# GCN passes: node columns looked up on TensorE from a table in two float32r parts instead of three bf16 parts

## The reference

```python
def gcn_conv(x, w, b, row, col, ew, n):
    h = x @ w
    deg = jax.ops.segment_sum(ew, col, num_segments=n)
    dinv = jnp.where(deg > 0, jax.lax.rsqrt(deg), 0.0)
    norm = dinv[row] * ew * dinv[col]
    out = jax.ops.segment_sum(norm[:, None] * h[row], col, num_segments=n)
    return out + b
...
x2 = jax.nn.relu(gcn_conv(x, w1, b1, row, col, ew, n))
x3 = jax.nn.relu(gcn_conv(x2, w2, b2, row, col, ew, n))
x4 = jax.nn.relu(gcn_conv(x3, w3, b3, row, col, ew, n))
```

## Time and profile before

| | |
|---|---|
| runs | 19631.51, 19641.05, 19712.04 us; median 19641.05 us |
| span of the profiled execution | 19593.6 us, 47 us below the median; the time beyond its span is not shown separately |
| instructions | 235897 |
| PE busy | 11895.5 us, 61% of the span |
| DVE busy | 10634.3 us, 54% |
| POOL busy | 9080.8 us, 46% |
| first GCN pass, width 16 | 11956 to 13408 us |
| second GCN pass, width 16 | 13489 to 14953 us |
| third GCN pass, width 32 | 15040 to 16870 us |

### The profile page before, as it was taken

One profiled execution on the slowest core, in us unless ns is written; L12 is line 12 of the kernel. 1 busy time (PEld: TensorE's weight loads), 2 busy tenths in 40 slices (PEclk: granted clock), 3 DMA queues, 4 the chain that ended last, 5 costly groups with the idle time before them and its releaser, 6 DMA issues. The chain is left out here.

```text
span 19593.6 us, 235897 instructions
## 1 busy us (share of the span) xinstructions
PE 11895.5 (61%) x70205; PEld 7895.5 (40%) x70205; DVE 10634.3 (54%) x24515; ACT 4354.8 (22%) x14847; POOL 9080.8 (46%) x9348
## 2 busy tenths in 40 slices
PE   4444445555546666666666446776776777566664
PEld 3333334444432222222222115665664333355453
DVE  5555545555544545555545794554554555356565
ACT  2333322333312222222222330000000111022221
POOL 4444434444445455455455103555444555444444
PEclk7777767777767777777777667887887888678777
DMA  2111112222212222222222671111111111022221
GB/s 62 58 58 58 58 48 75 77 76 76 77 55 64 69 65 70 69 65 70 69 65 70 214 260 31 32 32 29 31 32 29 34 34 34 23 56 57 58 56 48
DMA packets 637409, 1245.55 MB, mean 64 GB/s; under 512 B 206034, under 2 KB 390391, under 8 KB 586531
## 3 DMA queue, kind: packets, MB, share of 16 engines
q1 hardware_dynamic: 322624, 912.21, 13.3%
q0 software_dynamic: 300160, 269.02, 7.8%
q10 hardware_dynamic: 14337, 61.82, 0.8%
HBM read 475.84 MB, written 768.08 MB: 63 GB/s over the span
## 5 line engine op out<-in xcount | busy, mean ns | idle before, releaser
L1030 PE MATMUL p_slots<-part,one_lo 128*128 128x208 bf16 (+1 forms) x27048 | 3678.2, 296 | 1143.2 <-issue 992.4
L1341 PE MATMUL a_p_slots<-att_part,a_one_lo 128*128 128x455 bf16 x12348 | 2986.2, 389 | 1868.8 <-issue 1782.6
L1030 PEld LDWEIGHTS p_slots<-part,one_lo 128*128 128x128 bf16 x27048 | 2663.8, 105 | 2157.5 <-issue 1446.8
L990 POOL DMA_INDIRECT rows<-gcn_table,index x2450 | 2384.7, 973 | 2462.5 <-DVE p_msg L1109 1507.9
L1341 PEld LDWEIGHTS a_p_slots<-att_part,a_one_lo 128*128 128x128 bf16 x12348 | 1254.1, 102 | 3623.5 <-issue 2574.9
L1272 POOL DMA_INDIRECT sent<-a_out_rows,a_place x1568 | 1543.2, 984 | 2165.6 <-DVE a_run L1383 1688.3
L556 POOL DMA_INDIRECT msg<-x_rows,index x1372 | 1310.7, 955 | 1431.8 <-ACT index L574 1020.1
L1078 DVE TENSOR_TENSOR picked<-p_slots,one_hi 128x832 f32<-128x832 f32 (+1 forms) x588 | 708.2, 1204 | 2280.1 <-remote 1825.8
L556 POOL DMA_INDIRECT msg<-h_rows,index x1274 | 1225.8, 962 | 1533.0 <-ACT index L574 1174.2
L622 PE MATMUL p_slots<-x_part,key_lo 128*128 128x448 f32 x6916 | 1859.9, 429 | 121.6 <-DVE scratch L751 71.5
L1777 PE MATMUL e_p_slots<-soft_part,e_one_lo 128*128 128x456 f32 x5488 | 1429.0, 410 | 745.7 <-issue 674.4
(11 more groups left out here) (479 smaller groups left out, 18270.4 us busy)
## 6 DMA issues: line engine op xcount, KB each, us to landing
running_dst<-a_run SPq DMA_DIRECT2D x98, 1600.0 KB
running_src<-s_run SPq DMA_DIRECT2D x98, 1600.0 KB
running<-run SPq DMA_DIRECT2D x98, 1032.0 KB
running<-run SPq DMA_DIRECT2D x98, 1024.0 KB
running<-y SPq DMA_DIRECT2D x98, 656.0 KB
s_rows<-sent ACTq DMA_DIRECT2D x98, 584.0 KB
begun_x<-zeros SPq DMA_DIRECT2D x98, 512.0 KB
a_xdst<-begun_x SPq DMA_DIRECT2D x98, 512.0 KB
```

The costliest lines, as they stand in the source:

```text
L990: pool.indirect_dma_start(out=rows[h][:, KS[h] + k, :], out_offset=None, in_=table, in_offset=offsets(index[h][:, k:k + 1])).then_inc(gath ...
L1030: ins = nc.tensor.matmul(to, one_lo[h][:, q, e:e + P], flat(part[:, q, :, :]), start=q == 0 and part_no == 0, stop=q == CLASSES - 1 and pa ...
L1341: ins = nc.tensor.matmul(to[:, k, 0:Z * WIDE_CLASS], one_lo[h][:, q, e:e + P], flat(part[:, q, :, :]), start=q == 0 and part_no == 0, stop ...
```

## The change

The parts of the table become two of type float32r in place of three of type bf16, and the one-hots that multiply them become float32r too. The clearing of the padding is written through a float32 view. The loops over parts in `store_and_split` and `multiply` run over `parts`, so that they do two passes instead of three.

```diff
@@ store_and_split
-                step(nc.vector.memset(part[:, CLASSES - 1, :, J - FULL:CLASS], 0.0))
+                step(nc.vector.memset(part[:, CLASSES - 1, :, J - FULL:CLASS].bitcast(F32), 0.0))
@@ graph_pass
-        one_lo = by_half("one_lo", lambda h: [P, CLASSES, KS[h] * P], BF16)
+        one_lo = by_half("one_lo", lambda h: [P, CLASSES, KS[h] * P], F32R)
@@ convolve
-                    parts = [sb(f"part{k}_{n}", [P, CLASSES, c, CLASS], BF16, split) for n in range(3)]
+                    parts = [sb(f"part{k}_{n}", [P, CLASSES, c, CLASS], F32R, split) for n in range(2)]
```

## The result

The changed kernel takes 19517.15 us, the median of six runs (19482.72 to 19575.44), against 19646.17 us for the kernel before beside them (six runs, 19602.48 to 19712.04). The ratio is 0.9935 with a 95% interval of 0.9921 to 0.9949: faster by 0.65%, 128 us. The forecast had faster by 281 us. The sign was right, and more than half of the gain did not come. The profiled spans are 19593.6 and 19481.0 us, 112.6 us apart.

The account below looks back on a forecast made before the run. No engine near full; TensorE, VectorE and GpSimd nearly equally loaded without stalls, TensorE's stalls on top. Splits -13, width 16 -108, width 32 -160 make -281 us: 19,360 us, range 18,920 to 20,050.

Parts of the forecast that it names:

- Splits, -13 us: Table splits of the GCN passes: one rounding and one subtraction fewer per table, casts at no added cost, -13 us.
- Pace of the matmuls: TensorE's float32r look-up matmuls: 107 ns for 208 columns and 193 ns for 416, where bf16 takes 89 and 176.
- the dear short matmul: Rival at width 16: short float32r matmuls cost plain float32's 175 ns, 20,020 us; chance 0.21, a third of it still dearer.
- VectorE's one-hots: One-hots written as float32r on VectorE: +2.1 us a round at width 16, +1.5 us at width 32.
- Width 16, -108 us: Rounds of width 16 without stalls go from TensorE's 18.2 us to VectorE's 17.1: -1.1 us, 98 rounds, -108 us.
- Width 32, -160 us: Third pass: -4.9 us in every three steps, 98/3 times, -160 us; bounds -333 us and 0.
- the stalled step keeps its 16 us: Width 32, one step in three: the stall stays 16 us, the rest falls from TensorE's 12.7 to VectorE's 10.2, -2.5 us.
- the free pair: Width 32, the two unstalled steps of three: from 27.4 us to GpSimd's floor of 25.0 us for 20 gathers, -2.4 us.
- nothing measurable: Rival: VectorE's later product delays GpSimd's burst and the stall after it, refilling TensorE's saving; 19,600 us, chance 0.15.
- if the stalls lock differently to a shorter round: Closing caveat on TensorE's stalls, named as one way to be wrong above all; no size or chance given.
- The granted clock, a rival: TensorE's clock level as an explanation; not among the prediction's listed rivals, no size or chance given there.
- Shrinking with the count of matmuls: TensorE's "issue" stalls fall by a third with the matmuls, some -330 us beyond the full saving; 0.04 for more than that.

Follow-up runs that it names:

- the kernel with one gather: Changed kernel with only 1 of the 10 gathered columns of a step fetched at width 32, output incomplete: 18751.49 us, a round of 20.54 us.
- width 16 alone: Kernel before with two float32r parts only in the passes of width 16, three bf16 parts kept at width 32: 19497.57 us, ratio 0.9959.
- the two runs with five gathers: Changed kernel with 5 of 10 columns of a step gathered at width 32, output incomplete, run twice where nothing stalled: 13298.21 and 13333.61 us.
- the third part left out: Kernel before with two bf16 parts in place of three, looked-up values less exact: 19379.97 us, ratio 0.9906 to the kernel before.
- The kernels that should have tried this: Gathers released later, changed kernel 14204.45 us, kernel before 14243.65; changed kernel at width 32 with five gathers 13298.21, with half the matmuls 13479.03.

## Why the prediction was right in sign and wrong in size

*Splits, -13 us.* 3.2 us went from each table of 16 columns and 5.7 from that of 32 (2.73 and 3.00 us in the timeline before), 12 us. The casts cost the same in float32r, 1.53 us.

*Pace of the matmuls.* 208 columns: (6.50 - 0.25)/55 = 114 ns undisturbed, 107 predicted. 416 columns: 191 ns in the kernel with one gather, 193 predicted. The rival of the dear short matmul (134 ns and more) is out. The Trainium skill, "TensorE: Matmul & The Clock Gate", section "LDWEIGHTS (loading the stationary operand)", gives 107 ns for an ordinary load of 128 columns, and the pace measured at 208 columns stands 7 ns above that. That a load sets a floor for short matmuls fits the rows, 107 ns for 64 columns of plain float32 and 114 for 208 of float32r, but no run here separates the load from the rest.

*VectorE's one-hots.* 816, 752 and 638 ns for 800, 733 and 600 predicted. Its busy time in the first pass rose by 110 us for the 100 named.

*Width 16, -108 us.* Measured -0.8 us a round in the first pass and -1.1 in the second, and 105 - 9 (splits) = 96 us for both; the timed runs of width 16 alone give 80 us with its two splits. The size was right, by luck, since the reason, VectorE as bound without stalls, was not. The prediction had GpSimd's 15 gathers at 18.8 us, above TensorE's 18.2, and used such a bound at width 32 but not here: where no stalls were, the round went from 19.4 to 19.75 us (8277.1 to 9218.5 and 8253.7 to 9211.4 between the scans), because GpSimd was the bound, 15 x (0.997 + 0.30) = 19.5 us before and 15 x (1.020 + 0.30) = 19.8 after. The gain of width 16 was one of shorter stalled rounds only, and was no gain where nothing stalls. What made those rounds shorter was not tested; bursts joined there too, in 34 rounds of the first pass after for 7 before.

*Width 32, -160 us: the step that failed.* The prediction wrote that three steps hold one stall, that "the stalled step keeps its 16 us", and that the free pair gains 2.4 us and the stalled one 2.5. Measured: -0.2 us a round, -8 us over the pass in the trace, where -4.9 us in three steps makes -160. The stall nearly kept its length, 14 us in the stretch shown for 16; what did not stay was its frequency. With quicker steps, the next burst's release came before the burst in progress had ended, the bursts joined in pairs, and a stall came in every second step in place of every third. The quicker steps were handed back as stalls: late matmuls took some 565 us of the pass for 395. That is close to the rival "nothing measurable", whose mechanism (the stall after the burst moves with it) held at this width, while its cause, VectorE's later product, was the opposite of what happened: the product came earlier. The last sentence of the prediction named the case, "if the stalls lock differently to a shorter round", but gave it no price. It could have been had from rows 7 and the gathers' rows: with steps of 13.7 us against ten gathers at 1.25, there was a margin of about a microsecond before all bursts join.

*The granted clock, a rival.* It fell from 0.85 to 0.75 in the windows of the third pass. In the changed kernel it stands at 0.50 (the level of 1.2 GHz) from 15517 to 15522 us, behind a stall, where matmuls of 416 columns come every 347 ns, and at 1.00 (2.4 GHz) from 15527 to 15537, where they come every 190. Over the pass 567 matmuls came at the slower pace after and 347 before. With 347 - 190 = 157 ns for each after and 347 - 176 = 171 before that is 567 x 0.157 - 347 x 0.171 = 30 us more of TensorE's time, an estimate and a fifth of the missing 150. Where nothing stalls, the changed kernel has 535 such matmuls in the third pass and the kernel before none, and the rounds are alike; and the two runs with five gathers, at 0.79 and 0.92 in that pass, both have rounds of 20.8 us.

*What is shown and what is argued.* Shown: at width 32 the round doesn't follow the load of TensorE or VectorE (the third part left out), it does follow the gathers (one gather, 20.5 us), and without stalls it is GpSimd's 25.3 us in both kernels, in the kernel before TensorE's as well. Read from the traces only, though over all gathers of the passes: that a stall comes some 60 to 75 matmuls into an unbroken run and ends about 3 us behind it, and that joining makes stalls more frequent. The kernels that should have tried this met no stalls. What causes them stays open; since the same program ran with them and without, it takes something outside the kernel, and the gathers alone don't bring it. Shrinking with the count of matmuls was wrong: a third of the matmuls went, and "issue" rose in sum; its fall by 65 us at width 32 comes from the missing records.

## What to carry to other kernels

Before pricing a saving, divide a round by every engine's issue rate, GpSimd's included: here 20 gathers of 1.26 us were as long as the matmuls, so that lifting TensorE alone could give nothing, and moving one column across gave 0.7% where nothing stalled. A stall that is tied to another engine's bursts has a frequency as well as a length; ask whether a quicker step makes two bursts meet. And a saving measured on a disturbed chip can be another than on an undisturbed one: take the kernel before again beside each set of runs.

## What was not expected of the hardware

The same program took 19,600 us and 13,480 us, with and without idle time of TensorE that no wait explains: 4729 us of "issue" before its matmuls in the one profile and 0.2 us in the other. In the first, TensorE begins some 60 to 75 matmuls after GpSimd starts to gather, and then single ones, at width 32 mostly 1.4, 2.1 or 2.8 us apart, until the gathers pause.

GpSimd's gathers lengthen while VectorE writes one-hots. In the changed kernel, where nothing stalls, at width 16:

```profile
8702.64 0.94 POOL L990 DMA_INDIRECT rows<-gcn_table,index  x1 [0.30 <-issue]
...
8703.89 1.40 POOL L990 DMA_INDIRECT rows<-gcn_table,index  x1 [0.30 <-issue]
8705.59 1.15 POOL L990 DMA_INDIRECT rows<-gcn_table,index  x1 [0.30 <-issue]
8707.05 1.31 POOL L990 DMA_INDIRECT rows<-gcn_table,index  x1 [0.30 <-issue]
8708.67 0.94 POOL L990 DMA_INDIRECT rows<-gcn_table,index  x1 [0.30 <-issue]
```

```profile
8704.36 3.00 DVE L1048 TENSOR_SCALAR one_lo<-keys,lanes 128x1152 fp32r<-128x1152 f16 x4
```

Three gathers overlap the four one-hots and take 0.2 to 0.5 us more than the 0.94 us of the others; the two bf16 one-hot groups of the kernel before, 1.80 and 1.66 us long, stretch one or two each. This is where the 0.35 us a round of width 16 comes from when nothing stalls. The Trainium skill, "SBUF — State Buffer", section "Who interferes with whom", says that VectorE's tensor_scalar can run in a mode that takes the port which GpSimd needs, and that whoever comes second is blocked for the whole instruction. The trace agrees that a gather is held up, by 0.46 us at most here, less than one one-hot of 0.75 to 0.82 us; that it is blocked for a whole instruction no row shows. So one-hots of four bytes cost GpSimd time as well as VectorE, a term that the prediction did not have.
